# Token ranks with bf16 operands, and another hand-written timetable, in a cross-attention and mixture-of-experts kernel

## The reference, cut to what matters

```python
q, k, v = layernorm(x) @ Wq, ctx @ Wk, ctx @ Wv          # x: (16, 256, 128), ctx: (16, 1601, 128)
att = softmax(q @ k.T * 0.125)                            # per head: (256, 1601)
x = x + tanh(g0) * (att @ v) @ Wo.T
z = layernorm(x)
probs = softmax(z @ router_w.T)                           # 8 experts
top_p, top_i = top_k(probs, 2); top_p /= top_p.sum() + 1e-8
out = sum over the two experts e of top_p[e] * (gelu(z @ w1[e].T + b1[e]) @ w2[e].T + b2[e])
x = x + tanh(g1) * out
```

## Time and profile before

| | us | share of the span |
|---|---|---|
| median of 3 runs | 1379.92 | |
| the profiled execution | 1376.51 | |
| its span, first to last instruction | 1374.7 | |
| TensorE (PE) busy | 1318.8 | 96% |
| TensorE weight loads (PEld) | 639.0 | 46% |
| VectorE (DVE) busy | 1171.8 | 85% |
| ScalarE (ACT) busy | 1097.5 | 80% |
| GpSimd (POOL) busy | 550.0 | 40% |
| maxima, L1494, 1024 reductions | 987.5 | |
| exponentials, L1062, 1664 activations | 896.9 | |
| weighted sums, L791 | 534.1 | |
| scores, L743 | 458.5 | |
| windows, L765 | 451.1 | |
| mean granted TensorE clock | | 0.978 of full |

### The profile page before, as it was taken

One profiled execution on the slowest core, in us unless ns is written; L12 is line 12 of the kernel. 1 busy time (PEld: TensorE's weight loads), 2 busy tenths in 40 slices (PEclk: granted clock), 3 DMA queues, 4 the chain that ended last, 5 costly groups with the idle time before them and its releaser, 6 DMA issues.

```text
span 1374.7 us, 37718 instructions
## 1 busy us (share of the span) xinstructions
PE 1318.8 (96%) x13872; PEld 639.0 (46%) x13872; DVE 1171.8 (85%) x2239; ACT 1097.5 (80%) x2170; POOL 550.0 (40%) x1213
## 2 busy tenths in 40 slices
PE   5899999999999999999999999999999999999992
PEld 2333444444444444444444444444444433588882
DVE  7888999999998999999999999999999999355344
ACT  2378888989898888898988888888888888865551
POOL 3133335252626262535353535344443512145442
PEclk7699999999999999999999999999999999999997
DMA  3232121212121212121212122222211110387665
GB/s 114 66 95 72 48 68 48 71 46 73 44 74 49 74 44 79 38 66 50 62 55 62 57 60 62 58 65 58 63 55 40 49 35 6 103 245 220 192 205 201
DMA packets 65763, 109.14 MB, mean 79 GB/s; under 512 B 13660, under 2 KB 36572, under 8 KB 65436
## 3 DMA queue, kind: packets, MB, share of 16 engines
q1 hardware_dynamic: 58804, 94.33, 23.3%
q0 software_dynamic: 4544, 9.45, 2.1%
q10 hardware_dynamic: 2232, 2.96, 0.6%
HBM read 48.81 MB, written 14.64 MB: 46 GB/s over the span
## 4 chain that ended last, share of the span: by engine, by line
PE 84%; DVE 9%; DMA 2%; SPq 2%; issue 1%; ACT 1%; POOL 1%; ACTq 1%; POOLq 0%; DVEq 0%
PE pv L791 30%; PE mxp L765 16%; PE st L743 15%; DVE mx L1494 7%; PE st L1023 5%; PE mxp L1033 4%; PE st L863 4%; PE st L849 4%; SPq L380 1%; PE st L821 1%; PE st L875 1%; PE st L833 1%; PE st L898 1%; DMA arena<-results 1%; PE mxp L999 1%
## 5 line engine op out<-in xcount | busy, mean ns | idle before, releaser
L1494 DVE TENSOR_REDUCE mx<-mxp 128x2 f32<-128x804 f32 x1024 | 987.5, 990 | 68.9 <-PE mxp L765 54.7
L1062 ACT ACTIVATE arena<-st 128x512 f32<-128x512 f32 (+1 forms) x1664 | 896.9, 595 | 99.0 <-PE st L743 82.2
L791 PE MATMUL pv<-arena 128*32 128x256 f32 x6656 | 534.1, 393 | 0.4 <-ACT pv_sb L1069 0.4
L765 PE MATMUL mxp<-kpack,qpack 48*128 48x402 bf16 x2048 | 451.1, 343 | 20.3 <-DVE mx L1494 10.5
L743 PE MATMUL st<-qpack,kpack 51*128 51x256 bf16 (+1 forms) x3328 | 458.5, 273 | 0.8 <-DMA qpack<-mxT 0.7
L743 PEld LDWEIGHTS st<-qpack,kpack 51*128 51x128 bf16 (+1 forms) x3328 | 205.0, 96 | 207.3 <-ACT arena L1062 118.2
L765 PEld LDWEIGHTS mxp<-kpack,qpack 48*128 48x128 bf16 x2048 | 136.3, 94 | 171.0 <-DVE mx L1494 91.5
L791 PEld LDWEIGHTS pv<-arena 128*32 128x32 f32 x6656 | 131.5, 108 | 176.4 <-ACT arena L1062 92.9
L630 POOL CAST mxs<-nmx 128x8 bf16<-128x8 f32 x64 | 12.3, 192 | 312.6 <-DVE nmx L1502 312.4
L1198 ACT ACTIVATE arena<-st,bias 128x256 f32<-128x256 f32 x156 | 73.7, 475 | 56.5 <-PE st L1023 54.6
L673 POOL DMA_INDIRECT results<-ysb,idx x78 | 74.9, 961 | 88.1 <-PE st L1023 46.7
(11 more groups left out here) (184 smaller groups left out, 957.9 us busy)
## 6 DMA issues: line engine op xcount, KB each, us to landing
kpack<-ksp SPq DMA_DIRECT2D x762, 50.0 KB
arena<-in_ctxT SPq DMA_DIRECT2D x15, 800.5 KB, 4.7
arena<-in_w1T SPq DMA_DIRECT2D x39, 256.0 KB, 3.2
arena<-in_w2T SPq DMA_DIRECT2D x39, 256.0 KB, 3.3
qpack<-qsp SPq DMA_DIRECT2D x187, 32.0 KB
xblk<-rows SPq DMA_DIRECT2D x39, 132.0 KB, 2.3
rows<-in_pads SPq DMA_DIRECT2D x8, 264.0 KB, 3.9
qpack<-mxT SPq DMA_DIRECT2D x128, 3.0 KB
```

Source lines behind the costliest of these rows:

```text
L765: eng.matmul(mxp[pair % MX_BUFS][:, rg, 0:WIN], qpack[rows, b % 2, g * JJ + jj, t * P:(t + 1) * P], kpack[rows, b % 2, g * JJ + jj, WSTART ...
L791: ins = eng.matmul(pv[32 * j:32 * j + 32, 0:N], vaug[0:n, b % 2, kt, at:at + 32], pt[0:n, (2 * u + rg) % PT_BUFS, jj * N:(jj + 1) * N], st ...
L1062: eng.activation(pt[0:n, c % PT_BUFS, :], ring[bank_of["S", u, p]][0:n, :], ACT.Exp, scale=SCALE).then_inc(s_exp, 1)
L1494: eng.tensor_reduce(mx[:, tj, w, :], mxp[windows_done % MX_BUFS][:, :, 0:WIN], AX.X, ALU.max).then_inc(s_red, 1)
```

## The change

Masks and counts become bf16, with bf16 copies of the two constant matrices, which GpSimd makes once in its norm step for batch 0 (in batch 1 of the loop); the first `rank_tokens` waits for them on a new semaphore. Digits, places, lead and shortfall of the timetable are replaced.

```diff
-K_AT = {1: 0, 2: 1, 3: 2, 6: 3}
-V_AT = {13: 0, 14: 1, 27: 2, 32: 3}
-HEADS_AT = {5: 0, 35: 1}
+K_AT = {1: 0, 4: 1, 5: 2, 6: 3}
+V_AT = {25: 0, 26: 1, 27: 2, 28: 3}
+HEADS_AT = {2: 0, 42: 1}
...
-X_AT, Q_AT = 40, 42
+X_AT, Q_AT = 39, 43
...
-LEAD, SHORT = 28, 5
-WINDOWS_AT = ("1001101010111011111111000110111100011111101111101111",
-              "1210111110001110000001211011000111100000110000110000")
+LEAD, SHORT = 30, 7
+WINDOWS_AT = ("1011011110111111111111101001101110011111110111100111",
+              "1101111020000000000001101211100011100000011000120000")
...
-        mask = sb("mask", [P, NT, NE])
-        before = sb("before", [P, NT, NE])
+        mask = sb("mask", [P, NT, NE], BF16)
+        tri_bf, ones_bf = sb("tri_bf", [P, P], BF16), sb("ones_bf", [P, P], BF16)
+        before = sb("before", [P, NT, NE], BF16)
...
+        s_tri = sem("s_tri")
...
                     if b == 0:
                         eng.wait_ge(s_w2, 16 * N_W2)
+                        eng.tensor_copy(tri_bf[:, :], tri).then_inc(s_tri, 1)
+                        eng.tensor_copy(ones_bf[:, :], ones).then_inc(s_tri, 1)
                     eng.tensor_copy(xrow[:, :, :, TOK], tok[:, b * NT:(b + 1) * NT, :]
...
                 eng.wait_ge(*freed[i])
+                if b == 0:
+                    eng.wait_ge(s_tri, 2)
                 eng.wait_ge(s_base, b + 1)
                 dst = ring[i][:, 0:NT * NE]
-                eng.matmul(dst, tri, mask[:, :, :].rearrange("p t e -> p (t e)"), start=True, stop=False)
-                eng.matmul(dst, ones, before[:, :, :].rearrange("p t e -> p (t e)"), start=False,
+                eng.matmul(dst, tri_bf[:, :], mask[:, :, :].rearrange("p t e -> p (t e)"), start=True, stop=False)
+                eng.matmul(dst, ones_bf[:, :], before[:, :, :].rearrange("p t e -> p (t e)"), start=False,
                            stop=True).then_inc(s_rk, 1)
...
-                eng.matmul(ring[i][:, 0:NE], ones, before[:, 0, :], start=True, stop=True
+                eng.matmul(ring[i][:, 0:NE], ones_bf[:, :], before[:, 0, :], start=True, stop=True
                            ).then_inc(s_cntp, 1)
```

## The result

The changed kernel takes **1369.44 us** (median of 5 runs, 1368.17 to 1373.15), the kernel before beside it 1379.92 (5 runs): the ratio is 0.9929, 95% interval 0.9916 to 0.9942. That is 10.5 us faster, inside the range and of the forecast's sign, and little more than half of the 19 us forecast. The profiled execution took 1369.44, its span is 1367.6. The two spans differ by 7.1 us only, since the profiled execution of the kernel before ran 3.4 us under its median; the table accounts for these 7.1.

A forecast was written before the change was run, and what follows sets the result against it. PE bounds the kernel, by unit prices plus waits. Middle batch: 71.48 - 1.7 + 0.2 - 0.32 + 0.5 = 70.2 us; 18.2 over 14 batches plus 0.8 outside, 19 off 1379.92, gives 1361, range 1354 to 1373.

The forecast's parts named there:

- Bound and price of a unit: PE's time is additive: plain one-window unit 1.07 us, a further window 0.18; moving helpers changes nothing by itself.
- Ranks: L919 and L920 in bf16 instead of float32: 0.55 us falls to 0.23, saving 0.32 a batch; bounds 0 and 0.45.
- the row that I chose as nearest: Turning of the maxima (L804), also two bf16 matmuls, 0.23 us, taken as the price of bf16 ranks.
- Empty units: Plain units 29 and 48 without windows take 0.98 us instead of 0.89, set by ACT's exponentials: +0.2 us a batch.
- Waits: PE waiting for window buffers because VectorE is behind: the new table leaves 0.5 us a batch, a third of before.
- The old total of 1.7 us: Waits per batch in the old table, in units 16, 25, 29, 31, 33, 35, 42, 48 and elsewhere, put down to VectorE.
- the burst sums: VectorE against PE: units 24 to 28, 10.1 against 9.7 us; units 3 to 8, 10 against 10.5; no wait left.
- The rival of waits that move: Half or more of the old 1.7 us returns elsewhere; waits of 0.9 to 1.4 give 1366 to 1374 us; chance 0.22.
- Middle batch: One of 14 repeating batches between first and last: 71.48 us to fall to 70.2, sign 69.7 to 70.8.
- the 0.8 for ranks and counts of the tail: Saving outside the middle batches, from ranks and counts of the last batch and the tail: about 0.8 us in all.
- SP and the maxima rows: SP's queue places the maxima 32.8 us into the batch, 1.2 us to spare before unit 26: no cost.
- The line that I drew: Forecast counts as wrong if units 5 to 9 or 25 to 29 exceed their prices by over 0.5 us together.

The follow-up runs named there:

- VectorE quick: VectorE's reduction reads only half of each window: 1344.20 us on the changed kernel, 1357.28 us on the kernel before (one run each).
- windows lent earlier: Changed kernel with three windows moved to plainer units further off (27's to 23, 47's to 44, 8's to 18): 1382.88 us against 1379.33, ratio 1.0023.

## Why the prediction was right in sign and nearly twice too large

*Bound and price of a unit: right.* Lengths are those of the prices wherever nothing waits (1.07 plain, 2.15 and 2.33 with values, 2.11 with keys), and moving helpers in itself cost nothing.

*Ranks: 0.40 in their unit, 0.24 in the batch; forecast 0.32.* The two bf16 matmuls start 0.04 us apart and cost 0.15 (0.72 less 0.57) instead of 0.23, so the row that I chose as nearest was too dear. But PE then comes earlier to units 47 and 49, and waits there. I had this only as the bound "0 if VectorE is awaited". The Trainium skill ("TensorE: Matmul & The Clock Gate", LDWEIGHTS) would have given a saving of 0.34: nearer to 0.40 than mine, with 107 ns by its formula for 128 columns where the loads of these matmuls take 95 to 99. That columns alone set it does not hold for float32 here, where the loads of the same ranks' matmuls (128 columns) took 186 to 192 ns in the kernel before.

*Empty units: forecast +0.2, measured nothing.* Units 29 and 48 take 0.88 to 0.89. The earlier trace rows come from the last batch, and don't hold for these two.

*Waits: this step failed.* It had two errors. The old total of 1.7 us was put down to VectorE as a whole; with VectorE quick only 1.20 went, and about 0.5 stayed in units 33, 35 and 48, of which 35 and 48 are seen to wait for ScalarE's exponentials. And of VectorE's part I let 0.5 remain, where 1.03 did. The change took away 0.17 of it, not 1.2; the waits in 33 and 48, which are not VectorE's, went in its stead. The reason is in the burst sums: they set VectorE's total for five or six units against PE's, but VectorE sits idle inside the burst (0.98 us ahead of 660.14; 0.44, 0.21 and 0.29 us ahead of 631.26, 633.37 and 635.56), and is late at its end. From unit 29 on it is busy 98.6% of the time, so whatever is late there has nowhere to go. The rival of waits that move had the mechanism right and named the row for it; I gave it 0.22 and the forecast 0.48.

*Middle batch:* 70.62 is inside the 69.7 to 70.8 given as its sign, 0.42 over the forecast 70.2; that it isn't further off is partly luck. By the prediction's own sum, with the ranks at 0.40, the waits left are 70.62 - (71.48 - 1.7 - 0.40) = 1.24 us, 0.74 more than the 0.5 forecast, and the two errors the other way, the empty units (0.2) and the ranks (0.08), hide part of it. 1.24 is within the 0.9 to 1.4 of the rival, and the time within its 1366 to 1374. The 14 batches gave 12.1 us where 18.2 were forecast.

*The rest* of the 8.5 us missing is outside. There the spans grew by 5.0 us (0.7 + 1.8 - 0.4 + 2.9), where they were to fall by 0.8: the first batch grew by 1.8, forecast 0.4, and the 0.8 for ranks and counts of the tail can't be found under the tail's own spread of 4 us. Against that stand 3.4 us by which the medians are further apart than the spans, and no profile shows where they lie. The last batch's -0.4 came as said.

*SP and the maxima rows: right,* 33.1 against 32.8 us. The line that I drew, units 5 to 9 or 25 to 29 over their prices by more than 0.5 together, was not crossed (about 0.3 and 0.15, 28 over and 29 under), so it was drawn too wide: the waits were spread in tenths over 8, 28, 35, 47 and 49.

## What to carry to other kernels

Where two engines are within a few per cent of each other, don't balance sums over a stretch: walk through it buffer by buffer, since idle time of the second engine inside the stretch isn't given back. Before you credit a change with removing a wait, make the awaited engine quick in an experiment and see how much goes; part of it may belong to another one. In a table written by hand the lead, the places of helpers and the places of windows are one setting: each change of one alone here cost 0.4 to 3.3 us a batch. And ask of a gain what it is made of: only 0.17 of the 0.86 us here was less waiting for VectorE, which the table was meant to remove.

## What the runs showed of the hardware

Two bf16 matmuls with 128-column weights and 16 streamed columns start 0.04 us apart and cost 0.15 us in the stream of others (687.69 and 687.73, 0.72 less 0.57); in float32 they cost 0.55. A window's buffer is taken for well over its reduction: in the run with windows lent earlier PE began one at 655.71 us and got its buffer back at 657.36, 1.65 us, while VectorE reduced six windows without a gap at 0.93 each. One reduction takes 0.98 to 1.00 us in the timelines above, so some 0.65 of the 1.65 is left for the window's two matmuls and the hand-overs. With two buffers that caps what a burst can hold. TensorE's clock was at 2.4 GHz in one kernel and at 1.2 GHz in another at the same place in the first batch, after one wait of 0.84 us in the first and three of 0.22, 0.36 and 0.93 us in the second, and the same chunk of keys took 0.94 or 1.70 us. In a third (lead 28, heads moved) it stayed at 2.4 GHz (granted 1.00 from 60 to 70 us) after waits of 0.25, 0.36 and 0.93 us.
